# A two-layer adapter kernel: in the second layer, list rows loaded a step ahead and turned before the low-rank rows

## What is computed

```python
# layer 0
base_out = einsum('bsi,oi->bso', x, base_w) + base_b
res_hidden = einsum('bsi,ri->bsr', x, A)                 # rank 64
topw, topi = top_k(softmax(x @ router_w.T), 2)           # 2 of 16 experts
delta = einsum('bse,bsr,eor->bso', combine, res_hidden, B)
out = base_out + delta * SCALING
# layer 1
base = xf @ base_W.T
top_vals, top_idx = top_k(xf @ gate_W.T, 2)              # 2 of 28 experts
h = einsum('nd,erd->ner', xf, lora_A) * (gate * SCALING) # rank 8
out = base + einsum('ner,eor->no', h, lora_B)
```

## Time and profile before

| | |
|---|---|
| median of 3 runs | 1206.26 us (1205.31 to 1210.62) |
| profiled execution | 1202.36 us, its span 1200.5 us |
| TensorE (PE) busy | 98% of the span, 6819 products |
| ScalarE (ACT), VectorE (DVE), GpSimd (POOL) busy | 64%, 59%, 25% |
| granted TensorE clock | 0.997 of full speed, the 2.4 GHz level, throughout |
| DMA | 267 MB, mean 223 GB/s |
| list stage of layer 1 | about 606 to 870 us of the span, steps of about 22 us |

### The profile page before, as it was taken

One profiled execution on the slowest core, in us unless ns is written; L12 is line 12 of the kernel. 1 busy time (PEld: TensorE's weight loads), 2 busy tenths in 40 slices (PEclk: granted clock), 3 DMA queues, 4 the chain that ended last, 5 costly groups with the idle time before them and its releaser, 6 DMA issues.

```text
span 1200.5 us, 22121 instructions
## 1 busy us (share of the span) xinstructions
PE 1178.7 (98%) x6819; PEld 1040.0 (87%) x6819; DVE 706.7 (59%) x1985; ACT 767.7 (64%) x1746; POOL 298.0 (25%) x315
## 2 busy tenths in 40 slices
PE   8999899999999999999999999999999999999998
PEld 7999899999889899999788777787788888888887
DVE  6677677777556556457864444454445555565552
ACT  5666666665676867765567757767735755755752
POOL 4111733332223222234311122111131222222200
PEclk9999999999999999999999999999999999999999
DMA  8567555866899999987799999999975455555510
GB/s 303 210 234 265 201 214 189 309 240 207 214 325 318 307 326 309 326 294 217 164 234 288 284 290 306 278 292 306 266 177 106 114 123 106 121 122 106 121 53 35
DMA packets 84843, 267.17 MB, mean 223 GB/s; under 512 B 23264, under 2 KB 27488, under 8 KB 77504
## 3 DMA queue, kind: packets, MB, share of 16 engines
q1 hardware_dynamic: 72752, 230.12, 58.5%
q0 software_dynamic: 11600, 36.06, 16.9%
q10 hardware_dynamic: 432, 0.30, 0.1%
HBM read 154.24 MB, written 112.20 MB: 222 GB/s over the span
## 4 chain that ended last, share of the span: by engine, by line
PE 39%; DMA 9%; issue 1%; DVE 1%; SPq 1%; ACT 1%; POOL 0%; ACTq 0%; POOLq 0%; DVEq 0%
PE z L1470 11%; PE z L1471 11%; PE z L1472 11%; DMA x<-zs_dram,gpos 2%; DMA ht<-hs_dram 2%; DMA xin<-zs_dram,gpos 2%; DMA x<-x_dram 1%; DMA xin<-x_dram 1%; PE c L1470 1%; PE c L1472 1%; PE c L1471 1%; PE c L1551 1%; DVE xb L1442 1%; PE prep L1754 1%; ACT zt L763 0%
## 5 line engine op out<-in xcount | busy, mean ns | idle before, releaser
L763 ACT ACTIVATE moved<-mid 32x256 f32<-32x256 f32 x944 | 392.1, 415 | 137.3 <-DVE mid L1032 96.3
L1470 PE MATMUL z<-w_1h,yh 128*128 128x384 f32 (+1 forms) x512 | 190.1, 371 | 0.7 <-DVE w_1l L1140 0.7
L1470 PE MATMUL z<-w_0h,yh 128*128 128x384 f32 (+1 forms) x512 | 187.4, 366 | 0.2 <-DVE xb L1442 0.2
L1472 PE MATMUL z<-w_1l,yh 128*128 128x384 f32 (+1 forms) x512 | 185.8, 363 | 1.1 <-issue 1.0
L1472 PE MATMUL z<-w_0l,yh 128*128 128x384 f32 (+1 forms) x512 | 185.8, 363 | 0.0
L1471 PE MATMUL z<-w_1h,yl 128*128 128x512 f32 (+1 forms) x504 | 183.1, 363 | 0.4 <-issue 0.4
L1471 PE MATMUL z<-w_0h,yl 128*128 128x512 f32 (+1 forms) x504 | 182.8, 363 | 0.0
L674 POOL TENSOR_TENSOR carrier<-ones_col 128x1 f32<-128x1 f32 x96 | 24.1, 251 | 528.5 <-DMA xin<-zs_dram,gpos 116.6
L1470 PE MATMUL z<-w_2h,yh 128*128 128x252 f32 (+1 forms) x504 | 150.4, 299 | 1.0 <-DVE bd L1040 1.0
L1472 PE MATMUL z<-w_2l,yh 128*128 128x252 f32 (+1 forms) x504 | 150.0, 298 | 0.0
L1471 PE MATMUL z<-w_2h,yl 128*128 128x252 f32 (+1 forms) x496 | 147.4, 297 | 0.0
(11 more groups left out here) (225 smaller groups left out, 2603.0 us busy)
## 6 DMA issues: line engine op xcount, KB each, us to landing
bd<-bd_dram SPq DMA_DIRECT2D x96, 512.0 KB
zs_dram<-zt SPq DMA_DIRECT2D x96, 512.0 KB
hs_dram<-zt SPq DMA_DIRECT2D x34, 512.0 KB, 6.5
x8raw<-in_x_dram SPq DMA_DIRECT2D x32, 516.0 KB
xin<-in_x_dram SPq DMA_DIRECT2D x32, 512.0 KB, 7.5
x_dram<-xb SPq DMA_DIRECT2D x32, 512.0 KB
out_dram<-xb SPq DMA_DIRECT2D x31, 512.0 KB
bd_dram<-bd SPq DMA_DIRECT2D x8, 1024.0 KB
```

Of the source, the lines that this page charges most:

```text
L763: return nc.scalar.activation(o, i_, ACT.Copy)
L1470: T.matmul(o, ah, wh, start=start, stop=False, **kw)
L1472: return T.matmul(o, ah, wl, start=False, stop=stop, **kw)
```

## The change

In layer 1 only:

- The rows of list step s + 2 are loaded in the middle of the step that works on s, behind the stores 0 and 1 and ahead of bd loads 2 and 3. Before, the rows of s + 1 were loaded at the start of it, behind the x load. Those of step 13 are loaded at the end of `start_lists`, in t = 1.
- The two transposes stand between list pair 0 and the transposes of the low-rank rows, in t = 2 to 12. In t = 1 they stay ahead of the low-rank products.
- They write columns 256 to 511 of `prepp` (`HT1 = 2 * P`), and `ht_high` and `ht_low` read there.
- ScalarE waits for `hT_lo` of the tile ahead of `ht_high`.

Layer 0's list steps keep their order (`w == 0`, `two_ahead=False`, column 0).

```diff
--- before.py
+++ after.py
@@ -60,6 +60,7 @@
 SCALE0, SCALE1 = 32.0 / 64.0, 16.0 / 8.0
 ROUTE0, ROUTE1 = 12, 10
 TB = 4 * E0
+HT1 = 2 * P
 
 
 B0, B1 = 3 * P, HALF
@@ -469,9 +470,9 @@
                 for v in range(PER):
                     load_bd(WS * w, v, first=w == 0)
 
-            def listed_step(s, w, more):
-
-                if more:
+            def listed_step(s, w, more, two_ahead=False):
+
+                if more and w == 0:
                     load_ht(s + 1, w)
                 for group in ((0, 1), (2, 3)):
                     if more:
@@ -479,6 +480,8 @@
                             load_bd(s + 1, v)
                     for v in group:
                         store_zs(s, v, w)
+                    if two_ahead and group == (0, 1):
+                        load_ht(s + 2, w)
 
 
             load_x8(0, first=True)
@@ -582,7 +585,7 @@
                 sp.wait_ge(x1_stored[u], 16 * (TILES // 2))
             sp.wait_ge(a0.c_ps[1], TILES)
 
-            def step1(i, v, first=False, prefetch=True, start=False, lists=False, more=True):
+            def step1(i, v, first=False, prefetch=True, start=False, lists=False, more=True, two_ahead=True):
                 t = 4 * i + v
                 if prefetch:
 
@@ -592,8 +595,9 @@
                     load_xr(i + (v + 3) // 4, (v + 3) % 4)
                 if start:
                     start_lists(1)
+                    load_ht(WS + 1, 1)
                 if lists:
-                    listed_step(t - S1_LISTS + WS, 1, more)
+                    listed_step(t - S1_LISTS + WS, 1, more, two_ahead)
                 for b in range(2):
                     sp.wait_ge(a1.z_out[b], t + 1)
                     if at(t, TILES - 1):
@@ -609,8 +613,8 @@
             with sp.Fori(1, 3) as i:
                 for v in range(4):
                     step1(i, v, lists=True)
-            step1(3, 0, lists=True)
-            step1(3, 1, lists=True, more=False)
+            step1(3, 0, lists=True, two_ahead=False)
+            step1(3, 1, lists=True, more=False, two_ahead=False)
             step1(3, 2)
             step1(3, 3)
             with sp.Fori(4, TILES // 4 - 1) as i:
@@ -832,13 +836,13 @@
                 nc.scalar.activation(att[:, :], alg[:, :], ACT.Exp, bias=astat[:, 1:2],
                                      accum_out=astat[:, 2:3]).then_inc(att_exp, 1)
 
-            def ht_high(s, first=False):
+            def ht_high(s, first=False, at_column=0):
 
                 act.wait_ge(ht_ps, s + 1)
                 if not first:
                     act.wait_ge(zt_ps, PER * s)
                     act.wait_ge(hl_ready, s)
-                copy(hh[:, :, :].rearrange("p j r -> p (j r)"), prepp[:, 0:PER // 2 * P]).then_inc(hh_ready, 1)
+                copy(hh[:, :, :].rearrange("p j r -> p (j r)"), prepp[:, at_column:at_column + PER // 2 * P]).then_inc(hh_ready, 1)
 
             def outputs(s, v, banks, first=False):
 
@@ -993,7 +997,8 @@
                     outputs(s, 2, cp)
                     outputs(s, 3, tp)
                 if turn is not None:
-                    ht_high(turn)
+                    act.wait_ge(a1.hT_lo, t + 1)
+                    ht_high(turn, at_column=HT1)
 
             step1(0, 0, first=True, late=True)
             step1(0, 1, turn=WS)
@@ -1219,9 +1224,9 @@
                 mix_sum(t)
                 mix_low(t)
 
-            def ht_low(s):
+            def ht_low(s, at_column=0):
                 dve.wait_ge(hh_ready, s + 1)
-                V.tensor_tensor(hl[:, :, :].rearrange("p j r -> p (j r)"), prepp[:, 0:PER // 2 * P],
+                V.tensor_tensor(hl[:, :, :].rearrange("p j r -> p (j r)"), prepp[:, at_column:at_column + PER // 2 * P],
                                 hh[:, :, :].rearrange("p j r -> p (j r)"), ALU.subtract).then_inc(hl_ready, 1)
 
             step = [0]
@@ -1431,7 +1436,7 @@
                 if at(t, 0):
                     tiles_of_lists(1)
                 if turn is not None:
-                    ht_low(turn)
+                    ht_low(turn, at_column=HT1)
 
                 dve.wait_ge(x1_stored[u], 16 * (TILES // 2))
                 if not first:
@@ -1528,7 +1533,7 @@
                                          ident[:, :])
                     mm.then_inc(a0.y_ps[n], 1)
 
-            def turn_ht(s, first=False):
+            def turn_ht(s, first=False, at_column=0):
 
                 for v in range(PER):
                     pe.wait_ge(ht_in[v], 16 * s + 16)
@@ -1537,7 +1542,7 @@
                 else:
                     pe.wait_ge(hl_ready, s)
                 for j in range(PER // 2):
-                    mm = T.transpose(prepp[:, P * j:P * (j + 1)], ht[j][:, :], ident[:, :])
+                    mm = T.transpose(prepp[:, at_column + P * j:at_column + P * (j + 1)], ht[j][:, :], ident[:, :])
                 mm.then_inc(ht_ps, 1)
 
             def listed_pair(s, j):
@@ -1747,6 +1752,8 @@
                     pe.wait_ge(a1.c_out[1], t + 2)
                     pe.wait_ge(zt_out, PER * s)
                     listed_pair(s, 0)
+                if turn is not None and lists:
+                    turn_ht(turn, at_column=HT1)
                 pe.wait_ge(a1.hx, 2 * t + 2)
                 if tables:
                     pe.wait_ge(tab_ready, 4)
@@ -1772,8 +1779,8 @@
                 pe.wait_ge(a1.hT_lo, t + 1)
                 if first:
                     first_tiles(1)
-                if turn is not None:
-                    turn_ht(turn)
+                if turn is not None and not lists:
+                    turn_ht(turn, at_column=HT1)
                 if first:
                     pe.wait_ge(lb_lo, 2)
                 for b in range(2):
```

## The result

The changed kernel takes 1212.55 us (median of 6 runs, 1205.55 to 1219.70); the kernel before has a median of 1205.1 over six runs, three of them those of the 1206.26 above. The medians lie 7.5 us apart. The recorded ratio is 1.0081, with a 95% interval of 1.0048 to 1.0113, which is about 10 us. The forecast of 1205.4 is missed, and so is its range up to 1210.5, on the side that had 0.08.

A forecast was written before the change was run, and what follows sets the result against it. PE, 98% busy, was taken to set the time, with the DMA rings nearly full; -1.8 + 0.3 + 0.3 + 0.3 = -0.9 us took the profiled 1202.36 to 1201.5, and 3.9 to the median gave 1205.4 (range 1201.5 to 1210.5).

The forecast's parts named there:

- The waits removed: Layer 1 list steps: loading rows earlier removes PE's two late waits for them at the transposes, -1.8 us.
- The transposes moved: Moving the two transposes from step end to middle saves 0.17 and adds 0.20 us in 11 steps, +0.3 us.
- The first loads: Step 13's rows, loaded at the start of the lists, land at 618 against 618.16 when PE wants them, +0.3 us.
- SyncE's own delay: In SyncE's queue the moved issues delay bd loads about 1 us, harmlessly, and the x load +0.5 us at most.
- The rings: Small row packets passing ahead of x land it about 2 us later, leaving PE 0.2 us short in some steps, +0.3 us.
- 1.8 us of cover: On one late step, the time between xb's first half ending at 719.7 and PE's base product at 721.57.
- Never empty: In the second layer's list stage the 16 DMA engines, at a share of 1.05, were taken to be always occupied.
- The first, that the small loads push x back and PE pays: Rival: x lands 4 us late, not 2, costing PE 7 us in late list steps; 1212.4 us, chance 0.11.
- second: Rival: the rings are the bound, so PE loses the 1.8 us again waiting for xb or bd; 1206.6 us, chance 0.16.
- third: Rival: rows are late at the new place too, in step 2 by up to 2 us; 1207.6 us, chance 0.12.
- fourth: Rival: more comes back than seen, -3.7 us with the transposes' lower bound; 1202.6 us, chance 0.05.
- What would show it: Signs in the changed profile; wrong if new PE waits on xb, bd or ht exceed 2 us, or gain exceeds 4.

The follow-up runs named there:

- e1: The changed kernel run again with nothing edited; ratio 1.0069 to the kernel before.
- e3: The changed kernel with each moved row load bringing 16 of its 128 rows, same issues and order; ratio 1.0001 to the kernel before.
- e13: e5 with three unused table reads ahead of each x load, so x is issued 2.0 us later; ratio 1.0001 to the kernel before.
- e15: e3 with SyncE's loop over t = 4 to 11 written out; ratio 0.9997 to the kernel before.
- e6: Only the row loads moved, into two pairs of buffers, transposes at their old place, SyncE's loop written out; ratio 1.0068 to the kernel before.
- e2: The changed kernel with SyncE's loop over t = 4 to 11 written out, so no jump back; ratio 1.0058 to the kernel before.
- e8: The changed kernel with the x load issued ahead of the output store; ratio 0.9980 to the kernel before.
- e10: The kernel before with the x load ahead of the output store and SyncE's loop written out; ratio 1.0006 to the kernel before.
- e11: e8 with SyncE's loop written out; ratio 0.9998 to the kernel before.
- e12: e5 with the x load ahead of the output store; ratio 0.9991 to the kernel before.
- e7: The kernel before with its layer 1 row loads cut to 16 of 128 rows; ratio 0.9992 to the kernel before.
- e9: The kernel before with four unused table reads put in front of SyncE's loop over t = 4 to 11; ratio 1.0025 to the kernel before.
- e14: The kernel before with SyncE's loop written out, nothing else; ratio 0.9997 to the kernel before.
- e5: Only the transposes moved, row loads behind x as before, two pairs of buffers, SyncE's loop written out; ratio 0.9986 to the kernel before.

## Why the prediction was wrong

- **The waits removed, -1.8: right.** The late turns of before have no counterpart in after's stage or in e1's.
- **The transposes moved, +0.3: right.** In the middle, last list product to second base product, before and then after, and at the end, to the second low-rank product:

```profile
683.47 0.39 PE L1555 MATMUL t<-bd,hh 64*128 64x512 f32 x1
683.79 0.43 PE L1754 MATMUL prep<-ident,hx 128*112 128x128 f32 x2
683.98 0.48 PE L1470 MATMUL z<-w_1h,yh 128*128 128x512 f32 x1
684.29 0.40 PE L1471 MATMUL z<-w_1h,yl 128*128 128x512 f32 x1
```

```profile
682.99 0.39 PE L1560 MATMUL t<-bd,hh 64*128 64x512 f32 x1
683.31 0.44 PE L1545 MATMUL prep<-ident,ht 128*128 128x128 f32 x2
683.59 0.38 PE L1761 MATMUL prep<-ident,hx 128*112 128x128 f32 x2
683.72 0.47 PE L1475 MATMUL z<-w_1h,yh 128*128 128x512 f32 x1
684.03 0.39 PE L1476 MATMUL z<-w_1h,yl 128*128 128x512 f32 x1
...
690.63 0.39 PE L1560 MATMUL t<-bd,hh 64*128 64x512 f32 x1
690.95 0.50 PE L1475 MATMUL z<-lbh,h1h 112*128 112x512 f32 x1
691.29 0.40 PE L1476 MATMUL z<-lbh,h1l 112*128 112x512 f32 x1
```

  That is 1.04 us, 0.2 more than before (0.82), and 0.66 where it was 0.83: +0.03 to 0.05 a step; 0.20 and 0.17 were foreseen.
- **The first loads, +0.3: right within 0.3.** PE turned step 13's rows at 617.66 without a wait in after, and at 618.06 after 0.3 us of wait in e1.
- **SyncE's own delay, "+0.5 us at most": too small as a delay, right in that it wasn't priced.** SyncE in after's step 2:

```profile
622.14 5.72 SPq L451 DMA_DIRECT2D ht<-hs_dram  x4
628.62 1.77 SPq L457 DMA_DIRECT2D bd<-bd_dram  x2
630.43 1.06 SPq L461 DMA_DIRECT2D zs_dram<-zt  x2
631.60 0.52 SPq L607 DMA_DIRECT2D out_dram<-xb  x1
632.22 1.65 SPq L567 DMA_DIRECT2D x<-x_dram  x1
```

  The four row loads took 5.72 us and not 5, and started 0.7 us later; the bd loads left at 628.62 for 625.85, and x at 632.22 for 630.21, 2 us later. By e3, e13 and e15 that costs nothing measurable. The long jump back was not foreseen at all, since before's trace has none of it: 0 to 6.5 us by the pairs.
- **The rings, +0.3: here the prediction failed.** The moved loads by themselves cost some 8 us (e6, 1.0068 of before). The delay of x was about right (landing at 16.0 and 16.5 us for 14.7; 2 were forecast). Its price wasn't. The "1.8 us of cover" was read from one step of one execution, at the base product that waits for xb, and a shortfall of 0.2 us over "some steps" made +0.3. Three things were wrong with that. The wait comes at another place: the mixing products, which need x1h and `mixl`, stand ahead of xb's consumer, and 3.7 of after's 4.3 us are there. The small packets don't only push x back, they change which gather has large transfers beside it: the second grew by 1.5 us on the mean and by 2.9 at its longest. Counted from the start of GpSimd's row to the last packet, both gathers of the tile took over 11 us ahead of e1's three holes and of after's first. Ahead of after's second the first gather took 9.9, behind the x that landed at 19.2. (e2 has no jump; there the same load landed at 19.1, ahead of its hole of 4.6 us.) And a hole can cost more than its wait, for in e1 the clock behind two of them is at 0.50. A step with a hole takes 24.4 to 27.8 us where the others take 21.9; after has two of them, e1 three.
- **The reading of the rings.** "Never empty" was read from a mean share of 1.05. The slices of 643 to 644 of the kernel before have several of 0 and 1 tenths:

```profile
DMA  9933259959699895999293922249139900110999
```

  So the time that a set of small packets takes ("some 2 us") was read where the rings weren't full throughout, and e13 shows that a later issue need not be a later landing.
- **The rivals.** The first, that the small loads push x back and PE pays, gave 1212.4, and 1212.55 was measured. That the two agree so closely is luck: its 7 us were taken from between 2.2 and 11, and stood on 1206.26, where 1205.1 was measured beside the change; it asked for five late steps, and after's trace has two holes. That the moved loads are the cause is right (e3, e6). Its mechanism is so only in part: x lands 1.3 us later on the mean (1.8 in e1), not more than the 1.8 from which it was to decide, and ScalarE waits for x with its two gathers. Its chance of 0.11 rested on "most of the set passed in 2 us", which prices the set's own packets and not what is beside them. Rings that give the 1.8 us back and no more (second), late rows (third) and the larger gain (fourth) did not come about.
- **What would show it.** The text's own mark was new waits on xb, bd or ht of over 2 us; after has 4.3 us of new ones, but mostly on `mixl`, which it didn't list.

**Left open.** The experiments show that the loads' new place costs the time, and not by which way. Whether the holes come from x's displacement or from the company of the second gather was not separated: moving the packets moves both, and e8, e10, e11 and e12, by letting x pass the output store, change both too. That removing the `ht` waits lets PE come to the mixing products earlier, and so takes a little slack from the gathers, fits before, e7, e9, e10 and e14, which turn at the old place and wait on `ht` and nowhere else, and e5, which waits 3.0 us on `mixl`; it was not measured by itself.

## What to carry to other kernels

When the DMA rings are nearly full, a load that is moved forward can be paid by what it passes, and its bytes don't tell the price: here 128 KB a step, moved forward in ten steps, cost some 8 us. Ask which chain behind the passed transfers has the least slack, and read that slack at the first consumer on the bounding engine, over every step and over more than one execution, before calling it cover. Try giving the transfer that heads that chain its place back in the same edit: here x ahead of the output store turns 1.0069 into 0.9980, which is no gain over before, but no loss. And where a change puts instructions ahead of a loop of some hundreds, look at the time of its jump back.

## What the runs showed of the hardware

- SyncE's jump back over 332 instructions took 0.27 us, 5.5 to 7.2 us when 24 instructions more stood ahead of the loop (after, e1, e3), and 6.0 us with 12 more (e9).
- A wait of PE of 3.19 us in a stream that is 98% busy was followed, about a microsecond on, by 3.2 us at the lower clock level (e1). A wait of 1.89 us was followed by the lower level too in e6, and waits of 1.72 and 1.95 us were not in after.
- At a DMA share of about 1, x loads issued 2.0 us later landed no later: 11.6 us from issue to landing instead of 14.2 (e13 and e5, means of nine in one execution each).
- 128 KB in packets of 256 B, moved ahead of 3 MB of other transfers (two bd loads, two stores, the output store, x) in the order of issue in each step, cost 0.6 to 0.8% of the whole (after, e1, e2, e6); an eighth of the packets at the same place cost nothing measurable (e3, e15).
